# First slot stage of a hybrid block: moments of the Mamba rows taken two groups ahead, and the norm's bias added to x by GpSimd

## What is computed

```
x = x + mamba(layernorm(x))        # two Mamba layers, then a final layernorm with weight w and bias b
x = x + slots(layernorm(x))        # the stage of this change
x = x + window_attention(layernorm(x))
x = x + slots(layernorm(x))
```

## Time and profile before

| | us |
|---|---|
| median of 3 runs | 2447.85 (2445.73 to 2450.03) |
| the profiled execution | 2445.1, span 2443.3 |
| PE / DVE / ACT / POOL busy in the span | 2114.9 / 1886.0 / 1785.2 / 1636.1 |
| first slot stage, from its first load to its last matmul | about 1769.6 to 1914 |
| mean granted clock of PE in the span | 0.954 |

### The profile page before, as it was taken

One profiled execution on the slowest core, in us unless ns is written; L12 is line 12 of the kernel. 1 busy time (PEld: TensorE's weight loads), 2 busy tenths in 40 slices (PEclk: granted clock), 3 DMA queues, 4 the chain that ended last, 5 costly groups with the idle time before them and its releaser, 6 DMA issues. The chain is left out here.

```text
span 2443.3 us, 40627 instructions
## 1 busy us (share of the span) xinstructions
PE 2114.9 (87%) x14680; PEld 1256.1 (51%) x14680; DVE 1886.0 (77%) x2590; ACT 1785.2 (73%) x3059; POOL 1636.1 (67%) x1436
## 2 busy tenths in 40 slices
PE   5989899898988989899898989988527599999977
PEld 2545545454554545455454554544324367666655
DVE  6888889888898888889888898988566455556555
ACT  3989898988989898998889889898333144444442
POOL 2888989898898988889898898989622123112120
PEclk9999999999999999999999999999857789999989
DMA  7240413405052341414324051331050301111032
GB/s 240 61 122 14 121 58 78 107 25 122 18 122 65 105 109 31 122 44 96 81 51 114 17 122 51 88 88 43 10 186 0 128 19 38 32 35 32 21 124 69
DMA packets 129788, 183.75 MB, mean 75 GB/s; under 512 B 14002, under 2 KB 75954, under 8 KB 129204
## 3 DMA queue, kind: packets, MB, share of 16 engines
q1 hardware_dynamic: 129588, 181.16, 27.6%
HBM read 134.45 MB, written 42.47 MB: 72 GB/s over the span
## 5 line engine op out<-in xcount | busy, mean ns | idle before, releaser
L620 POOL TENSOR_TENSOR h<-h,C_rep 128x512 f32<-128x512 f32 x1024 | 1275.5, 1280 | 195.2 <-ACT h_carry L529 195.2
L404 DVE TENSOR_TENSOR_SCAN h<-decay,h_carry,psum 128x512 f32<-128x512 f32 x768 | 955.4, 1269 | 126.8 <-PE psum L751 95.7
L521 ACT ACTIVATE decay<-dt_rep,A 128x512 f32<-128x512 f32 x1024 | 729.1, 712 | 97.3 <-DVE h L404 93.9
L751 PEld LDWEIGHTS psum<-ident,u_B 128*128 128x128 f32 x4096 | 478.9, 142 | 558.5 <-DVE h L404 306.6
L751 PE MATMUL psum<-ident,u_B 128*128 128x128 f32 x4096 | 632.9, 281 | 137.5 <-DVE h L404 105.5
L543 ACT ACTIVATE u_B<-u_tok,B_tok 128x512 f32<-128x512 f32 x832 | 588.9, 709 | 64.0 <-PE psum L751 46.3
L404 DVE TENSOR_TENSOR_SCAN h<-decay,zero,psum 128x512 f32<-128x512 f32 x256 | 318.6, 1269 | 50.0 <-PE psum L751 34.5
L762 PE MATMUL psum<-h,state_sum 128*32 128x512 f32 x2048 | 282.6, 625 | 10.9 <-POOL h L620 10.5
L609 POOL TENSOR_TENSOR u_B<-u_tok,B_tok 128x512 f32<-128x512 f32 x192 | 200.3, 1043 | 19.1 <-DVE u_tok L375 19.1
L674 PE MATMUL psum<-x_dt_gated,tap_diag 128*128 128x512 f32 x384 | 189.2, 597 | 0.0
L1578 DVE TENSOR_REDUCE a_row_max<-a_psum 128x4 f32<-128x512 f32 x128 | 87.7, 685 | 127.3 <-PE a_psum L1719 127.3
(11 more groups left out here) (207 smaller groups left out, 2757.3 us busy)
## 6 DMA issues: line engine op xcount, KB each, us to landing
dt_rep<-dt_rows SPq DMA_DIRECT2D x256, 256.0 KB, 5.6
C_rep<-C_rows SPq DMA_DIRECT2D x256, 64.0 KB, 2.0
dt_rows<-x_dt_gated SPq DMA_DIRECT2D x32, 512.0 KB, 5.0
residual<-mamba_residual SPq DMA_DIRECT2D x16, 512.0 KB, 3.9
mamba_residual<-residual SPq DMA_DIRECT2D x16, 512.0 KB, 2.9
x_tok<-mamba_residual SPq DMA_DIRECT2D x15, 512.0 KB, 4.5
f_gru_weights<-in_slot_gru_dram SPq DMA_DIRECT2D x2, 2176.0 KB
u_B<-in_x_dram SPq DMA_DIRECT2D x8, 512.0 KB, 9.3
```

What stands on the lines that cost most here:

```text
L404: dve.tensor_tensor_scan(h[:, slot(u)], dec[:, u % DEC], PS[:, u % 2], first, ALU.mult, ALU.add)\
L521: act.activation(dec[:, u % DEC], dtr[:, k % EG], ACT.Exp, scale=A[:, s // STEPS, k:k + 1]).then_inc(S["decay"], 1)
L620: pool.tensor_tensor(h[:, slot(u)], h[:, slot(u)], crep[:, k // EG], ALU.mult).then_inc(S["hc"], 1)
L751: ins = pe.transpose(PS[:, u % 2, tb * P:(tb + 1) * P], pr[:, f % 2, tb, eg], ident[:])
```

## The change

All of it concerns the stage with `normed`; the second slot stage keeps its order.

- `R_AT` and `X_AT` give the moments new numbers: those of `r` are 0, 1, 3, 5 and those of the sum 2, 4, 6, 7.
- DVE takes the moments of `r` for groups 0 and 1 before anything else, those of group 2 before `combine(1)`, and those of group 3 before `combine(2)`.
- ACT does `norm_r(0)`, `norm_r(1)`, then `norm_x(0)`, and in the loop `norm_r(g + 2)` before `norm_x(g + 1)`.
- `x + b` leaves DVE: POOL does it for a whole group in one instruction (`add_bias`), with a semaphore `x_b` that DVE's `x + r` waits for.

```diff
+    R_AT = [max(2 * g - 1, 0) for g in range(G)]
+    X_AT = [min(2 * g + 2, 2 * G - 1) if normed else g for g in range(G)]
...
+                def add_bias(g):
+                    t = slice(TG * g, TG * (g + 1))
+                    pool.wait_ge(x_ld[g], 16)
+                    if g == 0:
+                        pool.wait_ge(x_ld[G], 16)
+                        pool.wait_ge(S["n_ld"], 16)
+                    pool.tensor_tensor(xa[:, t], xa[:, t], wb[:, 1:2].to_broadcast([P, TG, D]), ALU.add).then_inc(S["x_b"], 1)
...
                 for g in range(G):
-                    for n in range(PER * g, PER * (g + 1)):
-                        rstd(n)
+                    if normed:
+                        for r in range(2) if g == 0 else range(g + 1, min(g + 2, G)):
+                            if r == 0:
+                                add_bias(0)
+                            rstd(R_AT[r])
+                        if g + 1 < G:
+                            add_bias(g + 1)
+                    rstd(X_AT[g])
                     norm_x(g)
...
-                        dve.wait_ge(x_ld[g], 16)
                         if g == 0:
-                            dve.wait_ge(x_ld[G], 16)
                             dve.wait_ge(S["n_ld"], 16)
-                        dve.tensor_tensor(xa[:, t], xa[:, t], wb[:, 1:2].to_broadcast([P, TG, D]), ALU.add)\
-                            .then_inc(S["comb"], 1)
                         dve.wait_ge(S["rn"], g + 1)
...
-                        dve.wait_ge(S["comb"], 2 * g + 2)
+                        dve.wait_ge(S["comb"], g + 1)
+                        dve.wait_ge(S["x_b"], g + 1)
...
                 if normed:
                     r_moments(0)
+                    r_moments(1)
...
                 if normed:
-                    r_moments(1)
+                    r_moments(2)
                 combine(1)
-                if normed:
-                    r_moments(2)
                 dve.wait_ge(S["b2"], 1)
                 for g in range(G):
+                    if normed:
+                        r_moments(g + 3)
                     combine(g + 2)
                     top_k(g)
-                    if normed:
-                        r_moments(g + 3)
...
                 norm_r(0)
+                norm_r(1)
                 norm_x(0)
-                norm_r(1)
...
                     features(g)
+                    norm_r(g + 2)
                     norm_x(g + 1)
-                    norm_r(g + 2)
                     hidden(g)
```

More of the change, by code:

```diff
@@ L905, in slots @@
         PS = ctx.enter_context(nc.psum_tensor(tag + "psum", [P, 8, HALF], F32))
-        names = ("ident w_ld u_ld n_ld const ones slots s_tp s_feat mean c_mm c1 rt b2 stats ve rs nm rn comb xa xn xn_p tp "
+        names = ("ident w_ld u_ld n_ld half const ones slots s_tp s_feat mean c_mm c1 rt b2 stats ve rs nm rn comb x_b xa xn xn_p tp "
                  "xnT h_mm hT l_mm lg top shift rest ex mask es alpha a_tp aT slot_mm ws gi g_tp giT pre_mm pre wvo_mm wvo "
@@ L939, in _ @@
             def _(pool):
-                pool.memset(half[:], -0.5).then_inc(S["const"], 1)
+                pool.memset(half[:], -0.5).then_inc(S["half"], 1)
                 pool.memset(ones[:], 1.0).then_inc(S["ones"], 1)
                 pool.memset(xn[:, :, D:], 1.0).then_inc(S["ones"], 1)
-                pool.wait_ge(S["const"], 1)
+                pool.wait_ge(S["half"], 1)
                 def rstd(n):
@@ L949, in rstd @@
                     pool.tensor_tensor(nm[:, n], gm[:, n], rs[:, n], ALU.mult).then_inc(S["nm"], 1)
+                def add_bias(g):
[5 more added lines that the diff above has]
+                    pool.tensor_tensor(xa[:, t], xa[:, t], wb[:, 1:2].to_broadcast([P, TG, D]), ALU.add).then_inc(S["x_b"], 1)
                 def norm_x(g):
-                    n = PER * g + PER - 1
+                    n = X_AT[g]
                     pool.wait_ge(S["nm"], n + 1)
@@ L984, in r_moments @@
                     if g < G:
-                        moments(2 * g, rr, g, r_ld)
+                        moments(R_AT[g], rr, g, r_ld)
                 def combine(g):
@@ L1001, in combine @@
                             .then_inc(S["comb"], 1)
-                        dve.wait_ge(S["comb"], 2 * g + 2)
+                        dve.wait_ge(S["comb"], g + 1)
+                        dve.wait_ge(S["x_b"], g + 1)
                         dve.tensor_tensor(xa[:, t], xa[:, t], rr[:, t], ALU.add).then_inc(S["xa"], 1)
                         dve.wait_ge(S["xa"], g + 1)
-                        moments(2 * g + 1, xa, g, None)
+                        moments(X_AT[g], xa, g, None)
                     else:
@@ L1039, in weigh @@
                                       ALU.mult).then_inc(S["alpha"], 1)
-                dve.wait_ge(S["const"], 3)
+                dve.wait_ge(S["const"], 2)
                 if normed:
                     r_moments(0)
+                    r_moments(1)
                 else:
@@ L1110, in norm_r @@
                     if normed and g < G:
-                        n = 2 * g
+                        n = R_AT[g]
                         act.wait_ge(S["nm"], n + 1)
```

## The result

| | before | changed |
|---|---|---|
| median | 2446.51 us (6 runs, 2435.66 to 2450.03) | 2424.09 us (6 runs, 2420.97 to 2431.46) |
| ratio | | 0.9916, 95% interval 0.9892 to 0.9941 |
| profiled execution | 2445.1 us, span 2443.3 | 2420.97 us, span 2419.2 |
| first slot stage, first load's issue to end of the last matmuls | 144.40 us | 124.05 us |

The change is faster by 22 us of the median. Forecast were 14, with 7 to 21 as the range: the direction was right and the size was not, and 2424.1 lies 2.9 us under the range. The stage that was changed is 20.35 us shorter in the two profiles. The spans differ by 24.1; the rest is 0.5 us before the stage and 3.3 us in attention, to which the experiments come back.

The account below looks back on a forecast made before the run. The bound was taken as an open DVE, POOL, ACT, DVE round trip per group; group 3's variances 14.3 us earlier, less 0.3 or so for PE, gave 14 us less: median 2434 us, range 2427 to 2441.

Parts of the forecast that it names:

- POOL's power gets in between product and sum: +1.6 us.: DVE, groups 1 and 2: POOL's power for the next group's `r` delays DVE's sum by 1.6 us.
- The bias addition, 4.7 us.: POOL: one group's bias addition takes 4.7 us, bounds 4.2 to 5.1, and holds DVE's instructions to its end.
- the forecast's 1846.3: DVE, group 3: variances of the sum ready at 1846.3, where before it was 1860.65; 14.3 us earlier.
- Behind that the tail is as before.: PE, from group 3's last transposes on: same length as before, 1864.82 to 1875.55, clock 0.88.
- The rival "clock": PE's clock may rise sooner or fall; staying at 1.2 GHz leaves 7.3 us gained, 2440.5 us; chance 0.12.
- The last 0.3 us, for a PE that comes late: PE before group 3's transposes: ready at 1851.2 for 1850.5, 0.7 us late; 0.3 or so taken off the gain.
- the late start: Stage start: moments of group 1 at 1783.3, ACT's first norm at 1788.4 instead of 1781.56; group 0's variances 8.1 us later.
- group 1's product at the old place: DVE, group 1: multiplies at 1807.3 without a wait, where before it was 1807.42.
- no wait for ACT in groups 1 to 3: DVE: its 20.4 us wait for ACT's norm of `r` shrinks to the first group's.
- nothing measurable: Rival: POOL's addition at 7.9 us, or group 1's `r` landing 10 us later, leaves some 4 us gain, 2444; chance 0.08.
- slower: Rival: DVE's two-input instructions stretch POOL's addition over 9.4 us; at 11.5 us the kernel takes 2454; chance 0.05.
- Free: Rival: POOL's long additions don't hold up DVE; 21 us less, 2427; chance 0.13.

Follow-up runs that it names:

- the doubled power: Changed kernel with POOL's power for `r` of groups 2 and 3 made twice, the first into a spare tile; 2426.6 us, ratio 0.9929.
- after_shift: Changed kernel with 12 more dummy transposes on PE ahead of the stage's last matmuls; 2424.6 us, ratio 0.9918.
- no_bias: Changed kernel with every addition of b left out of the computation; 2422.6 us, ratio 0.9895.
- bias_only: Kernel before, in its old order, with only the bias addition moved from DVE to POOL; 2436.3 us, ratio 0.9974.

## Why the prediction was wrong in size

The forecast was 14 us for the stage, the stage gives 20.3, and the whole time agrees with the stage (22 and 15 us of the medians, 0.9916 and 0.9925). The 6.3 us are made of:

**"POOL's power gets in between product and sum: +1.6 us."** This step failed, in both groups to which it was applied. The row it rested on, 3.61 us for 1.64, shows POOL waiting for DVE; I turned it round, with the small L980 as the witness, which had met POOL's norms and not a power. In group 1 of the changed kernel the sum starts 0.03 us after the product's end with the power under way, and the doubled power leaves it there. In group 2 the sum starts as promptly, and the power comes only behind it. The rule of the Trainium skill (SBUF — State Buffer, SBUF: two separate sides), an exclusive lock for the whole instruction, fits the additions of 4.5 us, which held DVE's sum for 4.36 us in two runs. It doesn't fit the power, 1.65 us long.

**The bias addition, 4.7 us.** It took 4.49 to 4.53. In group 1 from product to variances it was 9.25 us, not 11.4: 1.6 us without the power, and L996 held for 0.9 us, not 1.5. In group 2 it was 11.12 for 11.4: there the power did cost, by another way. POOL's norms and its power stood behind DVE's product and sum, so the addition began only 1.7 us after the sum's end and held L996 for 2.7 us. With 0.5 us less at group 0 (31.9 for 32.4) this made group 3 ready 74.0 us after the first load, where the forecast's 1846.3 is 76.7: 2.7 of the 6.3 us.

**"Behind that the tail is as before."** The term was mis-sized by 3.3 us: from the last transposes to the end of the logits 9.07 for 10.73 us, and from there to the stage's end 36.8 for 38.5, of which the first gather is 1.6. The clock was at its upper level in both, for 0.88 and 0.68 before; why it was higher is not shown. The gather's part was luck: after_shift, the same program up to there, did not have it. The rival "clock" had been priced to the wrong side only: it said that it "may rise sooner", and gave no price for that. The last 0.3 us, for a PE that comes late, was not needed: PE waited 0.22 us for ACT. Its own working had 0.7 there, of which it took 0.3, and the 3.4 us of transposes "at the lower clock level" come from a row over which the clock rose; at the lower level alone 16 of them took 3.9 us.

What came out as said: the late start (moments at 1782.66 after a DMA wait, ACT's first norm of `r` at 1787.71, for 1783.3 and 1788.4 with a stage that began 0.5 us earlier), group 1's product at the old place (1806.34 for 1807.3), no wait for ACT in groups 1 to 3, L996 held behind POOL's additions, and the second addition at 1788.33 instead of 1789. The third came at 1810.97 instead of 1813.7, since the sum ahead of it was not delayed. The rivals "nothing measurable" and "slower" fall with the addition's 4.5 us. "Free" was wrong in its cause, for the long additions do hold DVE: it had group 3 ready after 69.2 us, which is near the 69.8 of no_bias and far from the 74.0 measured. That it came nearest in time is luck; 3.3 us from PE's clock, which it did not have, stood in for most of the difference.

## What to carry to other kernels

Look for the round trip that one engine waits out in the open for each tile, and take its first half one step further ahead: that alone was 14.5 of the 17.0 us by which DVE's last variances came earlier, while moving work off the waiting engine alone gave 1.4. A long two-input instruction on POOL costs DVE little where it falls beside the moments of a group, and up to its full length where it slips between two DVE instructions of two inputs; a wait that puts it behind the second is enough. Give the clock a price to both sides when PE's waits are taken away, and read a change ahead of PE at the last point before PE: behind it the same program gave 124.1 and 124.2 us for the stage in two profiles, and in a third it was 2.7 us behind at the end of the first gather.

## What was not expected of the hardware

- POOL's addition got ahead of DVE's sum by 0.01 us of start and held it for 4.36 us (6.65 for 2.29), twice, at different places.
- A DVE scaling with one SBUF input was held by it as well: L1054 took 3.50 us in bias_only and ended with POOL's addition, while the moments (L991) keep their 2.7 us beside one.
- A power of 8 columns on POOL, 1.65 us alone, was under way beside a DVE instruction with two SBUF inputs without delaying it, while it waited itself for the end of the one that had begun before it (3.61 us).
- One kernel's attention took 421.7 and 428.2 us in two profiles, the second with more moments of lower granted clock (0.97 in three windows of 50 us, for one).
- The same 32 matmuls took 3.70 to 5.38 us, at granted clocks from 1.00 down to 0.68; in after_shift they took 5.38 us in a program that was up to there the one that gave 3.70 twice.
